# The last 21 gathers of an index-driven copy into other homes, without pacing waits, and the token rows read back after the last turned pair

## The chip, the cores and the metric
One core of one Trainium2 chip runs the whole kernel as one program. The metric is the device time of that program in microseconds (us). The engines are named PE (TensorE, matmuls and transposes), DVE (VectorE), ACT (ScalarE), POOL (GpSimd) and SP (SyncE, which here only issues transfers).

## The reference, cut to what matters
A decoder block on x of 8 sequences, 256 positions, 256 features: a linear attention, then a cross attention with a table of relative positions, then a mixture of 8 experts. The change lies in the second part. It needs, for all pairs (v, m) of positions, the table row `rpe[hops[v, m]]`, and from it one product for each head and sequence:

```
pos_emb = rpe[hops]                                   # 256 x 256 rows of 256 floats
pe = pos_emb.reshape(Sq, Sq, NH, DH)
k_hop = jnp.einsum('bhvc,vmhc->bhvm', qh, pe)
qk = jnp.einsum('bhsd,bhtd->bhst', qh, k_scaled)
C = (qk + k_hop) * D
...
x = x + _L0_xattn_ref(_layernorm(x, axis=-1), ctx_1024, ctx_1024, ...)
```

The queries come from the first part's output x, which is also added at the end (the residual) and so must be kept until then.

## The kernel before, in words
**Stages.** From 0 to about 178 us PE computes the first attention, one sequence after another (the loops over b). From about 165 to 351 us it works on the table ("pairs", below). From 351 to about 425 us it does the cross attention in 16 units of 4.5 us each (u, half the heads of one sequence), and after that the router and the experts up to 752 us.

**Gathers.** The mask needed is triangular, so the 256 x 256 table rows are packed in 257 tiles n of 128 partitions and 256 floats. POOL fetches each with one indirect DMA (`gather`, L332: "in_rpe" is the table, "hopi" the indices), in the order that `tokens_gpsimd` and the loop after it in the block set. POOL runs its instructions in order, so a gather whose wait is not met holds all that follow.

**Homes.** `rows_of(n)` says where tile n lands. There are 142 first homes: spare room in PET, U and E1 (tiles 0 to 39), 86 slots of G (40 to 125), and the 16 rows of X (126 to 141, `NKEPT`). X holds the token rows x; each pair of its rows is stored to HBM (`kept_dram`, "tokens_kept", semaphore `x_st`) before a gather may overwrite it. The tiles from 142 on reuse homes: 142 to 149 rows of U, 150 to 235 the G slots, and 236 to 256 the G slots 65 to 85 a third time. `last_in(n)` is the tile that lay in n's home before.

**Pairs.** PE turns tiles in pairs q (tiles 2q and 2q+1) with four transposes (`turn_pair`, L1031), which raise the semaphore `turned`; DVE and ACT copy them from PSUM to PET by turns, and PE multiplies them with the queries four pairs later (`products`, L2102). "turned >= k" means that pairs 0 to k-1 are turned. PE goes through pairs in order and waits for the landing of both tiles of a pair.

**Pacing.** Besides the wait for its home, each gather has a second one. In the loops over b it stands behind some step of PE (`gather_behind`); in the loop at the end of the block it waits for `turned >= min(evenly, n // 2 - LEAD)`, `evenly` being a straight line from pair 7 up.

**Tokens back.** SP waits for turned >= 71 (all tiles in X are turned), and reads X back from HBM in one DMA of 2 MB (semaphore `x_ld`). After that come in SP's order: four loads of the running maximum (`run_max`, 512 KB each, into "Dm" tiles in G), each behind a count of turned pairs; the context of two sequences; then, when the last product is done, five small loads (semaphore `m_ld`), and the loads of the cross attention.

**Who needs X and the small loads.** `mlstm_gpsimd`: POOL masks the Dm tiles (`mask(u)`, L1181), ACT takes their exponentials (`decay(u)`, L1403), DVE multiplies. Between `mask(2)` and `mask(3)` POOL waits for `x_ld` and for `m_ld` (before L1226, which changes one of the small loads); the first sum into X comes 14 us later.

Of the kernel before, what the change touches and what calls it, by code (L numbers as in the profile page):

```python
# [16 lines left out]
B, S, D = 8, 256, 256  # L17
# [24 lines left out]
NBLK = 257  # L42
# [5 lines left out]
LEAD = 6  # L48
# [66 lines left out]
def build(nc, x_d, ctx_d, ctxr_d, idx_d, cst_d, wqT_d, wkT_d, wvT_d, woT_d, wk_d, gw_d, sw_d, wg_d, gb_d,  # L115
          rpe_d, lnw_d, lnb_d, rng_d, rnb_d, rw_d, rb_d, lg_d, lb_d, w1_d, b1_d, w2_d, b2_d, out_d):
    ctx = ExitStack()
    with ctx:
# [155 lines left out]
        def rows_of(n):  # L274
# [21 lines left out]
            if n < NFULL:  # L296
                k = n - NSPARE
            elif n < NFIRST + NAGAIN + NBUF:
                k = n - NFIRST - NAGAIN
            else:  # L300
                k = THIRD_AT + n - NFIRST - NAGAIN - NBUF
# [11 lines left out]
        def last_in(n):  # L313

            if n < NFIRST + NAGAIN:
                return LATE + n - NFIRST
            if n < NFIRST + NAGAIN + NBUF:
                return n - NFIRST - NAGAIN + NSPARE
            return NFIRST + NAGAIN + THIRD_AT + n - NFIRST - NAGAIN - NBUF
# [39 lines left out]
        def tokens_gpsimd(pool):  # L359
# [19 lines left out]
            for b in range(-1, B + 1):  # L379
                new, now, old = b + 1 < B, 0 <= b < B, b >= 1  # L380
# [31 lines left out]
                if b == B:  # L412
                    for q in range(2, NTURNED - 1):
                        gather_behind(turned, q)
                if now:
                    gather_behind(av_d, NU * b + 4)
                if b == B:
                    gather_behind(qt_full, B)
# [692 lines left out]
        def mlstm_sync(sp):  # L1111
# [22 lines left out]
            context(1)  # L1134
            sp.wait_ge(prod, products_done(NPAIR - 1))
# [910 lines left out]
        with nc.Block(no_gpsimd_drain=True) as block:  # L2046
            @block.sync
            def _(sp):
                tokens_sync(sp)

                sp.wait_ge(r_M_r, 1)
                sp.dma_start(m_dram, r_M).then_inc(r_dma, 16)
                sp.wait_ge(turned, (NFIRST - 1) // 2 + 1)
                sp.dma_start(X[:, 0:NKEPT, :], kept_dram).then_inc(x_ld, 16)
                sp.wait_ge(r_dma, 16)
                mlstm_sync(sp)
                experts_sync(sp)

            @block.gpsimd
            def _(pool):  # L2060
                rest = tokens_gpsimd(pool)
                for i, n in enumerate(rest):

                    evenly = NTURNED + 1 + i * (NPAIR - LEAD - NTURNED) // len(rest)
                    if n < NFIRST:
                        pool.wait_ge(x_st, 16 * ((n - NFULL) // 2 + 1))
                        pool.wait_ge(turned, min(evenly, n // 2 - LEAD))
                    else:
                        pool.wait_ge(turned, max(last_in(n) // 2 + 1, min(evenly, n // 2 - LEAD)))
                    gather(pool, n)  # L2070
# [209 lines left out]
```

## Time and profile before

| what | us |
|---|---|
| median of 3 runs (lowest, highest) | 752.5 (751.54, 754.65) |
| time of the profiled execution | 754.1 |
| its span in the trace | 751.9 |
| PE busy in the span | 723.6 |
| POOL busy in the span | 452.3 |
| first and last gather start | 3.62 and 344.21 |

The profile's span begins at the first instruction and ends with the last. All times in the rows below are us from the span's start unless they say otherwise. PE's clock is granted by a throttle; "PEclk" of 1.00 is full speed. A row's "idle before" names what ended the idle time of that engine before the instruction; "issue" there means that the engine waited for nothing that the profile shows.

### The profile page before, as it was taken

The numbers are of one execution on the slowest core, as the hardware profiler recorded it, in microseconds if no ns is written. First come the engines' busy times: TensorE is split into PE (matmuls) and PEld (weight loads), VectorE is DVE, ScalarE is ACT, GpSimd is POOL, SyncE is SP. The second block draws the span as 40 slices with busy tenths as digits, with TensorE's granted clock in tenths as the row PEclk, the third lists the DMA queues.
The fourth block names the chain that finished last, engine by engine and source line by source line (L and its number), as shares of the span: only waits on it lengthen the run. The fifth ranks groups of instructions, "written<-read, shape, count | busy, mean of one in ns | idle before, by whom it ended". The sixth has DMA issues, their size and how long they took to land.

```text
span 751.9 us, 17208 instructions
## 1 busy us (share of the span) xinstructions
PE 723.6 (96%) x5868; PEld 652.5 (87%) x5869; DVE 394.8 (53%) x1003; ACT 365.5 (49%) x944; POOL 452.3 (60%) x522
## 2 busy tenths in 40 slices
PE   8999999988999999988999989999999999999996
PEld 4667777768999999987999966999999999999995
DVE  2567666675856534433999993333333333333331
ACT  2334444334766534435999664434434344343441
POOL 6767777776877777775776541444454444544442
PEclk8999999999999999999999999999999999999999
DMA  8434444443333375643898996121212222122221
GB/s 294 132 94 129 131 135 136 138 135 95 92 99 102 104 217 158 158 128 82 266 255 216 304 362 210 29 42 35 35 35 35 39 38 35 35 35 40 37 35 22
DMA packets 75812, 88.29 MB, mean 117 GB/s; under 512 B 11952, under 2 KB 66032, under 8 KB 75632
## 3 DMA queue, kind: packets, MB, share of 16 engines
q0 software_dynamic: 19824, 43.93, 23.9%
q1 hardware_dynamic: 52256, 40.11, 18.0%
q10 hardware_dynamic: 3680, 3.54, 1.4%
q8 instruction: 34, 0.56, 0.3%
q14 instruction: 18, 0.15, 0.1%
HBM read 75.82 MB, written 11.73 MB: 116 GB/s over the span
## 4 chain that ended last, share of the span: by engine, by line
PE 81%; issue 5%; POOL 5%; DVE 5%; DMA 3%; ACT 1%; SPq 0%; DVEq 0%; POOLq 0%; ACTq 0%
PE ps L1795 19%; PE ps L1803 18%; PE ps L2102 10%; PE ps L1031 5%; POOL G L332 4%; PE ps L485 4%; PE ps L1301 3%; PE ps L552 2%; PE ps L526 2%; PE ps L478 2%; PE ps L1303 2%; PE ps L576 1%; PE ps L450 1%; PE ps L1784 1%; PE ps L1283 1%
## 5 line engine op out<-in xcount | busy, mean ns | idle before, releaser
L332 POOL DMA_INDIRECT G<-in_rpe,hopi x193 | 188.0, 974 | 65.1 <-issue 54.0
L1860 ACT ACTIVATE G<-ps,U 128x128 f32<-128x128 f32 x312 | 84.9, 384 | 161.6 <-PE ps L1795 161.6
L1795 PEld LDWEIGHTS ps<-G,QT 128*128 128x128 f32 x1248 | 145.3, 192 | 1.9
L1795 PE MATMUL ps<-G,QT 128*128 128x128 f32 x1248 | 145.5, 275 | 0.0
L1803 PE MATMUL ps<-G 128*128 x624 | 141.0, 379 | 0.0
L1803 PEld LDWEIGHTS ps<-G 128*128 128x128 f32 x624 | 115.6, 190 | 14.2
L2102 PE MATMUL ps<-U,PET 128*128 128x128 f32 (+3 forms) x768 | 100.6, 275 | 0.0
L2102 PEld LDWEIGHTS ps<-U,PET 128*128 128x128 f32 x768 | 94.4, 194 | 0.1
L979 DVE COPY PET<-ps 128x512 f32<-128x512 f32 x64 | 44.2, 691 | 84.9 <-PE ps L1031 83.4
L1739 POOL DMA_INDIRECT out<-G,slots x39 | 71.3, 1829 | 24.0 <-issue 24.0
L2145 ACT ACTIVATE PET<-ps 128x512 f32<-128x512 f32 (+1 forms) x63 | 37.4, 594 | 84.6 <-PE ps L1031 81.1
L2007 DVE TENSOR_SCALAR G<-ps,U 128x128 f32<-128x128 f32 x78 | 28.4, 406 | 83.1 <-PE ps L1784 83.1
L1031 PE MATMUL ps<-cst,G 128*128 128x128 f32 x386 | 59.5, 277 | 4.2 <-DMA G<-in_rpe,hopi 4.2
L1716 POOL DMA_INDIRECT G<-hidden_rows,slots x39 | 40.0, 1027 | 35.1 <-issue 15.1
L1745 POOL TENSOR_TENSOR U<-cst 128x1 f32<-128x1 f32 x37 | 8.0, 215 | 85.3 <-DMA out<-G,slots 85.3
L677 ACT ACTIVATE U<-ps 128x512 f32<-128x512 f32 (+2 forms) x56 | 28.7, 512 | 55.2 <-PE ps L478 29.8
L1031 PEld LDWEIGHTS ps<-cst,G 128*128 128x128 f32 x386 | 46.3, 148 | 4.9 <-DMA G<-in_rpe,hopi 4.9
L2037 DVE SCALAR_TENSOR_TENSOR G<-ps,U,G 128x256 f32<-128x256 f32 x39 | 18.9, 484 | 59.1 <-PE ps L1803 59.1
L810 DVE TENSOR_TENSOR U<-ps,cst 128x1024 f32<-128x1024 f32 x32 | 38.3, 1219 | 13.8 <-PE ps L552 8.2
L332 POOL DMA_INDIRECT U<-in_rpe,hopi x38 | 38.3, 1007 | 11.6 <-issue 11.0
L1844 ACT ACTIVATE QT<-U 128x1024 f32 x39 | 43.2, 1109 | 2.4 <-issue 2.4
L1995 DVE TENSOR_SCALAR QT<-U 128x1024 f32 x39 | 27.1, 694 | 28.5 <-issue 28.5
(250 smaller groups left out, 1254.3 us busy)
## 6 DMA issues: line engine op xcount, KB each, us to landing
G<-run_max SPq DMA_DIRECT2D x16, 512.0 KB, 7.5
U<-in_w SPq DMA_DIRECT2D x16, 512.0 KB, 7.5
G<-in_w SPq DMA_DIRECT2D x8, 1024.0 KB, 12.4
G<-in_rpe,hopi POOLq DMA_INDIRECT x193, 2.9
U<-in_ctx SPq DMA_DIRECT2D x8, 256.0 KB, 2.8
tokens_kept<-X SPq DMA_DIRECT2D x8, 256.0 KB, 2.4
X<-tokens_kept SPq DMA_DIRECT2D x1, 2048.0 KB, 11.6
hidden_rows<-QT ACTq DMA_DIRECT2D x8, 256.0 KB, 6.8
```

Of the source, the lines that this page charges most:

```text
L332: pool.indirect_dma_start(out=dst, out_offset=None, in_=rpe_d, in_offset=bass.IndirectOffsetOnAxis(ap=hopi[:, n:n + 1], axis=0)) \
L810: nc.vector.tensor_tensor(am[n % 2], s, tri.unsqueeze(1).unsqueeze(1).to_broadcast([P, 4, 2, P]), ALU.mult).then_inc(am_r, 1)
L979: copy(PET[:, q % NPT, 0:w], bank(turn_bank(q), 512)[:, 0:w]).then_inc(pet_r[q % 2], 1)
L1031: mm = pe.transpose(o[:, n % 2, j, :], src[:, j * P:(j + 1) * P], ident)
L1716: pool.indirect_dma_start(out=z_in[u], out_offset=None, in_=z_dram, in_offset=bass.IndirectOffsetOnAxis(ap=tokg[:, u:u + 1], axis=0)) \
L1739: pool.indirect_dma_start(out=out_d, out_offset=bass.IndirectOffsetOnAxis(ap=tok[:, u:u + 1], axis=0), in_=ysb[u], in_offset=None, bounds_ ...
L1795: mm = pe.matmul(bank(1 + 2 * u + c // 4, 4, P)[:, c % 4], w1c[u][:, k, c], hT[u][:, k, :], start=(k == 0), stop=(k == KC - 1))
L1803: mm = pe.matmul(bank(6 + u, D), gel[u][:, c, :], w2s[:, one(e), c, :].rearrange("p o n -> p (o n)"), start=(c == 0), stop=(c == NI - 1))
L1844: nc.scalar.activation(w1c[u][:, 1], w1_of(e, 1), ACT.Copy) \
L1860: ins = nc.scalar.activation(gel[u][:, c, :], bank(1 + 2 * u + c // 4, 4, P)[:, c % 4], ACT.Gelu, bias=b1c[u][:, c:c + 1])
L2102: mm = pe.matmul(o, pet[:, n % 2, j, :], rhs, start=True, stop=True, skip_group_check=True)
L2145: return nc.scalar.activation(out, src, ACT.Copy)
```

## The change
It has three parts. (1) Tiles 236 to 251 land in the 16 rows of X, and only 252 to 256 in G slots (65 to 69). (2) The loop over b on POOL ends one turn earlier, so that the gathers it issued in the turn b = B come in the plain loop, and that loop has no `evenly`: a gather waits for its home alone. (3) SP reads X back after all 129 pairs are turned, behind the contexts and ahead of the five small loads.

```
             elif n < NFIRST + NAGAIN + NBUF:
                 k = n - NFIRST - NAGAIN
+            elif n < NFIRST + NAGAIN + NBUF + NKEPT:
+                return X[:, n - NFIRST - NAGAIN - NBUF, :]
             else:
-                k = THIRD_AT + n - NFIRST - NAGAIN - NBUF
+                k = THIRD_AT + n - NFIRST - NAGAIN - NBUF - NKEPT
             return G[:, k * D:(k + 1) * D]
...
             if n < NFIRST + NAGAIN + NBUF:
                 return n - NFIRST - NAGAIN + NSPARE
-            return NFIRST + NAGAIN + THIRD_AT + n - NFIRST - NAGAIN - NBUF
+            if n < NFIRST + NAGAIN + NBUF + NKEPT:
+                return NFULL + n - NFIRST - NAGAIN - NBUF
+            return NFIRST + NAGAIN + THIRD_AT + n - NFIRST - NAGAIN - NBUF - NKEPT
...
-            for b in range(-1, B + 1):
-                new, now, old = b + 1 < B, 0 <= b < B, b >= 1
+            for b in range(-1, B):
+                new, now, old = b + 1 < B, 0 <= b, b >= 1
...
-                if b == B:
-                    for q in range(2, NTURNED - 1):
-                        gather_behind(turned, q)
                 if now:
                     gather_behind(av_d, NU * b + 4)
-                if b == B:
-                    gather_behind(qt_full, B)
...
             context(0)
             context(1)
+            read_until(NBLK - 1)
+            sp.dma_start(X[:, 0:NKEPT, :], kept_dram).then_inc(x_ld, 16)
             sp.wait_ge(prod, products_done(NPAIR - 1))
...
-                sp.wait_ge(turned, (NFIRST - 1) // 2 + 1)
-                sp.dma_start(X[:, 0:NKEPT, :], kept_dram).then_inc(x_ld, 16)
...
-                for i, n in enumerate(rest):
-
-                    evenly = NTURNED + 1 + i * (NPAIR - LEAD - NTURNED) // len(rest)
+                for n in rest:
                     if n < NFIRST:
                         pool.wait_ge(x_st, 16 * ((n - NFULL) // 2 + 1))
-                        pool.wait_ge(turned, min(evenly, n // 2 - LEAD))
                     else:
-                        pool.wait_ge(turned, max(last_in(n) // 2 + 1, min(evenly, n // 2 - LEAD)))
+                        pool.wait_ge(turned, last_in(n) // 2 + 1)
                     gather(pool, n)
```

On POOL, at tiles 125 to 133, the order before is this (L332 is the gather; the names in brackets are the semaphores that it waits for, "gathered" the landing of a gather 40 tiles earlier, "gate_full" PE's last product of the first attention):

```order
L332 DMA G<-in_rpe,hopi 128x256 [waits ct_full]
L332 DMA X<-in_rpe,hopi 128x256 [waits gathered3,x_st,out_full]
L332 DMA X<-in_rpe,hopi 128x256 [waits x_st,turned]
L332 DMA X<-in_rpe,hopi 128x256 [waits gathered4,x_st,turned]
L332 DMA X<-in_rpe,hopi 128x256 [waits x_st,turned]
L332 DMA X<-in_rpe,hopi 128x256 [waits gathered5,x_st,qt_full]
L332 DMA X<-in_rpe,hopi 128x256 [waits x_st,gate_full]
L332 DMA X<-in_rpe,hopi 128x256 [waits gathered6,turned,x_st]
L332 DMA X<-in_rpe,hopi 128x256 [waits turned,x_st]
```

and of the change, the same nine tiles:

```order
L336 DMA G<-in_rpe,hopi 128x256 [waits x_st]
L336 DMA X<-in_rpe,hopi 128x256 [waits gathered3,x_st]
L336 DMA X<-in_rpe,hopi 128x256 [waits x_st]
L336 DMA X<-in_rpe,hopi 128x256 [waits gathered4,x_st]
L336 DMA X<-in_rpe,hopi 128x256 [waits x_st]
L336 DMA X<-in_rpe,hopi 128x256 [waits gathered5,x_st]
L336 DMA X<-in_rpe,hopi 128x256 [waits x_st]
L336 DMA X<-in_rpe,hopi 128x256 [waits gathered6,x_st]
L336 DMA X<-in_rpe,hopi 128x256 [waits x_st]
```

No gather has moved; the waits for PE are gone, and only those for the stored token rows stay.

On SP, from the store of the running maximum to the last small load, before (m_dram is "run_max"):

```order
L2052 DMA run_max<-U 64x256 [waits r_M_r]
L2054 DMA X<-tokens_kept 128x16x256 [waits turned]
L1127 DMA G<-run_max 128x4x256 [waits turned,r_dma]
L1127 DMA G<-run_max 128x4x256 [waits turned] x3
L1115 DMA G<-in_ctx 128x256 [waits turned]
L1116 DMA G<-in_ctxr 128x256
L1115 DMA G<-in_ctx 128x256
L1116 DMA G<-in_ctxr 128x256
L1138 DMA PET<-in_lnw 128x256 [waits prod]
L1138 DMA PET<-in_rw 128x2x8
L1138 DMA PET<-in_rng 128x2
L1138 DMA PET<-in_rnb 128x2
```

and of the change:

```order
L2053 DMA run_max<-U 64x256 [waits r_M_r]
L1126 DMA G<-run_max 128x4x256 [waits turned,r_dma]
L1126 DMA G<-run_max 128x4x256 [waits turned] x3
L1114 DMA G<-in_ctx 128x256 [waits turned]
L1115 DMA G<-in_ctxr 128x256
L1114 DMA G<-in_ctx 128x256
L1115 DMA G<-in_ctxr 128x256
L1135 DMA X<-tokens_kept 128x16x256 [waits turned]
L1139 DMA PET<-in_lnw 128x256 [waits prod]
L1139 DMA PET<-in_rw 128x2x8
L1139 DMA PET<-in_rng 128x2
L1139 DMA PET<-in_rnb 128x2
```

The 2 MB read of X went past eight loads, and now stands right ahead of the small loads.

## Rows read from the trace of the kernel before

**Rows 1.** The page: busy us and share of the span of each engine.
```profile
PE 723.6 (96%) x5868; PEld 652.5 (87%) x5869; DVE 394.8 (53%) x1003; ACT 365.5 (49%) x944; POOL 452.3 (60%) x522
```

**Rows 2.** The chain that ended last, near the last gathers (start, length, what).
```profile
336.71 0.95 POOL G L332
337.65 0.30 issue
337.96 3.85 DMA G<-in_rpe,hopi
```

**Rows 3.** POOL's instructions in order of time, at tiles 131 and 132.
```profile
177.02 1.44 POOL L332 DMA_INDIRECT X<-in_rpe,hopi  x1 [1.64 <-PE ps L596]
181.06 0.94 POOL L332 DMA_INDIRECT X<-in_rpe,hopi  x1 [2.61 <-PE ps L1031]
```

**Rows 4.** PE's instructions in order of time, at pairs 12 and 13.
```profile
187.59 0.60 PE L1031 MATMUL ps<-cst,U 128*128 128x128 f32 x4
...
188.91 0.60 PE L1031 MATMUL ps<-cst,U 128*128 128x128 f32 x4
```

**Rows 5.** PE's instructions in order of time, pairs 121 to 128.
```profile
331.53 0.66 PE L1031 MATMUL ps<-cst,G 128*128 128x128 f32 x4
...
335.69 0.66 PE L1031 MATMUL ps<-cst,G 128*128 128x128 f32 x4 [0.96 <-DMA G<-in_rpe,hopi]
...
346.09 0.63 PE L1031 MATMUL ps<-cst,G 128*128 128x128 f32 x4
...
347.45 0.38 PE L1031 MATMUL ps<-cst,G 128*128 128x128 f32 x2
```

**Rows 6.** Busy time in three stretches: PE, PEld, DVE, ACT, POOL, PEclk, DMA share, GB/s.
```profile
331.50:341.80 10.30, 6.12 (x50) 5.44 (x48) 2.09 (x4) 1.89 (x5) 7.66 (x9) 1.00 0.37 106
341.80:346.00 4.20, 4.15 (x24) 4.16 (x25) 0.69 (x1) 0.73 (x2) 3.48 (x5) 0.59 0.36 101
266.00:276.00 10.00, 10.00 (x94) 10.00 (x92) 4.37 (x7) 4.00 (x9) 7.56 (x9) 1.00 0.99 314
```

**Rows 7.** DMA issues: line or tensors, count, KB each where fixed, us from issue to landing.
```profile
G<-in_rpe,hopi POOLq DMA_INDIRECT x193, 2.9
...
X<-tokens_kept SPq DMA_DIRECT2D x1, 2048.0 KB, 11.6
out<-X SPq DMA_DIRECT2D x1, 2048.0 KB, 7.8
X<-in_x SPq DMA_DIRECT2D x1, 1536.0 KB, 16.5
out<-X SPq DMA_DIRECT2D x1, 128.0 KB, 8.6
PET<-in_rb SPq DMA_DIRECT2D x1, 4.0 KB, 2.9
```

**Rows 8.** SP's issues in order of time: start, length of the issue.
```profile
5.54 8.54 SPq L349 DMA_DIRECT2D U<-in_ctx  x1
...
177.66 0.37 SPq L357 DMA_DIRECT2D tokens_kept<-X  x1
...
353.26 0.43 SPq L1138 DMA_DIRECT2D PET<-in_rb  x1
...
451.25 0.38 SPq L1703 DMA_DIRECT2D out<-X  x1
451.68 3.09 SPq L1704 DMA_DIRECT2D out<-X  x1
```

**Rows 9.** POOL's instructions in order of time, last gather to mask(3).
```profile
344.21 0.95 POOL L332 DMA_INDIRECT G<-in_rpe,hopi  x1 [0.30 <-issue]
...
356.31 0.87 POOL L1226 TENSOR_SCALAR PET<-PET 128x256 f32<-128x256 f32 x1 [3.53 <-DMA PET<-in_rb]
357.26 2.81 POOL L1181 TENSOR_SCALAR_AFFINE_SELECT G<-G 128x512 f32<-128x512 f32 x2
```

**Rows 10.** ACT's instructions in order of time: first of decay(3).
```profile
361.50 0.50 ACT L1403 ACTIVATE G<-G,AT 128x256 f32<-128x256 f32 x1
```

## The prediction
> **What bounds the kernel now.** I read the page first: PE is busy 96% of the span, POOL 60% [rows 1]. By shares alone gathers would be free. The chain of waits says otherwise for one stage: near the end of the table stage it leaves PE and runs back through POOL, gather after gather, 0.95 us each with 0.30 us between them [rows 2]. So a tile costs POOL 1.25 us and a pair 2.5 us. PE needs less for a pair: turning pair 12 and pair 13 begins 1.32 us apart [rows 4]. PE begins far behind POOL (it turns pair 12, tiles 24 and 25, at 187.59, and POOL had begun tile 132 at 181.06 [rows 3, 4]) and catches it up at the end. In PE's own order of time this is seen from pair 122 on: it turns pair 121 at 331.53 and pair 128 at 347.45, 15.92 us for seven pairs that would take 7 x 1.32 = 9.2 us [rows 5]. The missing 6.7 us are idle time before the turns, ended by the landing of a gather, and a stretch of 4.2 us at a granted clock of 0.59, the lower of the two levels, which followed 10.3 us in which PE was busy for 6.1 [rows 6]. The last gather starts at 344.21 [rows 9], and the last turn (one tile) follows 3.2 us later. So the end of this stage moves with POOL's last gather, and what comes behind it, the cross attention, starts from there.
>
> **Part 2, the waits taken away.** I looked for every gather whose idle time is over 0.30 us and is ended by PE. In the part that the change touches there are two: tile 131, which stood 1.64 us behind gate_full, and tile 132, which stood 2.61 us behind turned >= 7 [rows 3]. All later ones, 124 of them, show 0.30 or 0.31 us: their paced waits are met when POOL comes. Taken away: (1.64 - 0.30) + (2.61 - 0.30) = 1.34 + 2.31 = 3.65 us. Do other waits step in? x_st: the last two of the 16 rows of X are stored about 180 us (SP issues that store at 177.66 [rows 8]), and their tiles 140 and 141 come eight and nine places behind tile 132, now at 181.06 - 3.65 = 177.41, so not before 177.41 + 8 x 1.25 = 187.4. Tile 142 needs turned >= 13; pair 12 is turned at 187.59 + 0.60 = 188.2, and POOL comes to that tile at 177.41 + 10 x 1.25 = 189.9 or later. From tile 150 on the need grows by one pair in two gathers (2.5 us) while PE makes a pair in 1.32 us. None of them holds POOL. So the last gather starts at 344.21 - 3.65 = 340.56. The bounds: 3.3 to 4.0, since some gathers take 1.3 to 1.6 us instead of 0.95 (tile 131 took 1.44, [rows 3]), and which ones do will be others.
>
> **Part 1, the new homes.** Before, tiles 236 to 256 waited for turned >= 108 to 118 or the pacing, and were never held. Into X they need turned >= 64 to 71, long past; tiles 252 to 256 need turned >= 108 to 110, some 20 pairs before PE's place. One gather costs the same whatever its home. This part is worth nothing by itself; 0 us. It only matters that X is now in use to the end, which forces part 3.
>
> **What PE makes of it.** PE's own pace would bring pair 128 at 331.53 + 9.24 = 340.8, the gathers bring it at 347.45 - 3.65 = 343.8: still bound by POOL, so all of the 3.65 arrives. PE now meets POOL some three pairs later and idles about 3 us rather than 6. The stretch at the low clock cost a little that showed: the last gather, with the median landing of 2.9 us [rows 7], was there at 344.21 + 2.9 = 347.1, and its turn began at 347.45 [rows 5], since PE was still at work that had piled up. If the clock holds, 0.35 more: about 4.0 us for the end of the stage.
>
> **Part 3, the tokens back late.** It now starts when pair 128 is turned: the turn ended at 347.45 + 0.38 = 347.83 before [rows 5], so 343.8 now. It lands in 7.8 us if it is like the other 2 MB transfer that ran alone, the store at the end, or in 11.6 us as this very transfer did before [rows 7], when the gathers ran beside it and the transfer engines were busy for 0.99 [rows 6]. No gather is left in flight by 343.8 + 0.5, so I take 8.0: 351.8. The five small loads come behind it on SP's queue. In the pair of stores at the end the second, of 128 KB, was held 3.09 us at its issue and landed at 451.68 + 8.6 = 460.3, 1.2 us after the first (451.25 + 7.8 = 459.05) [rows 7, 8]. So the small loads land at 351.8 + 1.2 = 353.0. Before, the last of them landed at 353.26 + 2.9 = 356.2 [rows 7, 8], 4.0 earlier would be 352.2: they are 0.8 us late. Who waits for that? POOL does L1226 and mask(3), which ended at 357.26 + 2.81 = 360.07 [rows 9]; queued behind it are the masks 4 and 5. ACT took mask(3)'s tile at 361.50 [rows 10], so 1.4 us are free. 0.8 fits in: cost 0, and I take 0.3 for the run_max loads that are also queued behind the 2 MB. If that cover were gone each us more would cost one us, since POOL, ACT, DVE and PE pass the units on in 4.5 us steps without slack. The bounds: with 11.6 us X lands at 355.4, the small loads at 356.6, 4.4 late, cost 3.0.
>
> The Trainium skill has a rule that speaks against this part: by "DMA: Bandwidth & Descriptors", section "Two DMAs through the same engine are not ordered", descriptors of one queue on one transfer engine start in order. By it the small loads cannot pass the 2 MB; the two stores at the end agree with it. Its fit in the section "Anatomy of one DMA" (2.0 us and the bytes over 436 GB/s, given for transfers issued by POOL) makes an estimate of 6.8 us for X, which would leave the small loads in time; the row's 7.8 is used.
>
> **Sum.** -3.65 (waits) - 0.35 (clock) + 0.3 (late loads) = -3.7 us. Against the profiled execution: 754.1 - 3.7 = 750.4 (span 748.2). That execution was 1.6 us above the median of the three; against the median it is 752.5 - 3.7 = 748.8.
>
> **Rivals.**
> 1. The tokens land late (as before, in 11.6 us, or SP is held at their issue): net -4.0 + 1 to 3, so 749.5 to 751.5. For it: the 8.54 us in which SP was held behind the loads at the start [rows 8]. Against it: nothing else moves then.
> 2. The clock falls where it hurts. Before, the low stretch lay where PE would have waited for gathers anyway. If PE's idle time of 3 us before pairs 126 to 128 brings such a stretch on, it lies over the last products and the first unit. Its 4.2 us at 0.59 take 0.41 x 4.2 = 1.7 us, which then all show: -3.65 + 1.7 + 0.3 = -1.65, so 750.9. Against it: the idle share is smaller than the 4.2 of 10.3 us before.
> 3. Nothing comes of it: POOL's gathers, set off against DVE's work, lose the 3.65 us again in longer ones, 752.5. Against it: the work beside them is periodic and the same.
> 4. Slower: X takes as long as the 1.5 MB of tokens at the start, 16.5 us [rows 7]. Then it lands at 360.3, the small loads at 361.5, 9.3 late, cost 7.9, net +3.9: 756.4. It decides from the point at which the small loads land over 5.4 us late (1.4 of slack and the 4.0 won), that is when X takes 12.4 us or more. Against it: at the start it shared the transfer engines with the other first loads, and now it has them nearly alone.
>
> **How the numbers follow.** Chances: the forecast 0.60, rival 1 0.16, rival 2 0.11, rival 3 0.05, rival 4 0.08. The forecast's own range is -3.0 to -4.2, with 0.7 us for the spread of medians (three runs spread over 3.1): 747.6 to 750.2. To hold 8 in 10 it must reach over most of rivals 1 and 2, so 747.4 to 752.0. A change of this kernel under 0.5% (3.8 us) can hardly be told from none. The forecast stands nearly on that line: 0.41 for faster, of the forecast a little under 0.7; within 0.5% is the rest of it with rivals 1 to 3, 0.52; slower is most of rival 4, 0.07.
>
> **What would show it.** In the profile after: no idle time over 0.3 us before the gathers of tiles 131 and 132; last gather at 340.6; pair 128 turned at some 343.5; at most three turns that wait for a gather; X issued at 343.8 and landed within 9 us; mask(3) done before ACT's decay(3) asks for it, so that the cross attention starts 4.0 us earlier. Wrong it would be if POOL showed new waits for turned or x_st, if L1226 began later than 353.8, or if PE's clock were low after 344.

## The result, and the profile after

| | before | after |
|---|---|---|
| median (lowest to highest), 6 runs each | 751.5 us (748.28 to 754.65) | 746.9 us (743.68 to 747.93) |
| profiled execution | 754.1 us | 746.76 us |
| its span | 751.9 us | 744.6 us |

The ratio on record is 0.9921, 95% interval 0.9902 to 0.9940: 5.9 us saved, between 4.5 and 7.4. The two medians of six differ by less, 4.6 us. The forecast was 748.8 us in a range of 747.4 to 752.0 and a saving of 3.7 us. The direction was right; the measured 746.9 lies 0.5 us below the range, 1.9 below the forecast. Of these 1.9 us, 1.0 is the base (the median of the kernel before was 752.5 with three runs and is 751.5 with six), and the rest a saving that was forecast too small. On two further chips, on which the kernel before itself takes 810 to 811 us, the same change costs 58 and 61 us; that is told with the experiments.

**The page.** PE is busy for 4.3 us less, POOL for as long as before; compare [rows 1].

```profile
PE 719.3 (97%) x5868; PEld 650.1 (87%) x5869; DVE 394.9 (53%) x1003; ACT 365.2 (49%) x944; POOL 452.1 (61%) x522
```

**POOL in order of time, after**: tiles 131, 132, 142, and the last gather (idle time before each in brackets).

```profile
174.07 0.95 POOL L336 DMA_INDIRECT X<-in_rpe,hopi  x1 [0.30 <-issue]
175.32 0.95 POOL L336 DMA_INDIRECT X<-in_rpe,hopi  x1 [0.30 <-issue]
...
187.82 0.95 POOL L336 DMA_INDIRECT U<-in_rpe,hopi  x1 [0.30 <-issue]
...
337.59 0.95 POOL L336 DMA_INDIRECT G<-in_rpe,hopi  x1 [0.30 <-issue]
```

The waits of 1.64 and 2.61 us of [rows 3] are gone, as announced, and no gather behind them waits. But the last gather [rows 9] comes 6.62 us earlier (344.21 - 337.59), not 3.65. Where is the other 2.97? Tile 131 stood at 177.02 with a wait of which 1.34 was removed, so 175.68 was expected for it, and it comes at 174.07: 1.61 us were won ahead of everything that the change touches. The page's windows show where: between 41 and 46 us, in the first attention, which is the same code in both kernels, PE ran at a granted clock of 0.66 in the execution before and at full clock in the one after (first row before, second after). By tile 40, at 55.96 us before and 54.37 after, the 1.6 us are complete, and they stay the same up to tile 130.

```profile
41.00:46.00 5.00, 4.36 (x25) 2.93 (x26) 2.51 (x6) 1.34 (x3) 2.98 (x4) 0.66 0.30 86
```

```profile
41.00:46.00 5.00, 4.58 (x35) 3.65 (x36) 3.77 (x9) 2.24 (x5) 3.78 (x5) 1.00 0.36 107
```

The rest, 1.36 us, is in the gathers' own length. POOL's groups over the same 132 gathers, tiles 125 or 126 to 256, before and then after (busy us, mean ns; idle us):

```profile
L332 POOL DMA_INDIRECT G<-in_rpe,hopi x108 | 107.1, 991 | 32.9 <-issue 29.9 <-PE ps L1031 3.0
L332 POOL DMA_INDIRECT X<-in_rpe,hopi x16 | 17.3, 1079 | 8.5 <-issue 3.7 <-PE ps L1031 3.2 <-PE ps L596 1.6
L332 POOL DMA_INDIRECT U<-in_rpe,hopi x8 | 9.8, 1230 | 2.4 <-issue 1.8 <-PE ps L1031 0.6
```

```profile
L336 POOL DMA_INDIRECT G<-in_rpe,hopi x92 | 92.0, 1000 | 28.0 <-issue 26.2 <-PE ps L1030 1.8
L336 POOL DMA_INDIRECT X<-in_rpe,hopi x32 | 31.7, 989 | 9.8 <-issue 9.4 <-DMA tokens_kept<-X 0.3
L336 POOL DMA_INDIRECT U<-in_rpe,hopi x8 | 9.2, 1145 | 2.4 <-issue 1.5 <-PE ps L1030 0.9
```

Before they were busy for 107.1 + 17.3 + 9.8 = 134.2 us, after for 92.0 + 31.7 + 9.2 = 132.9: 1.3 us less. The traces tell which: before, tiles 131, 138 and 139 took 1.44, 1.58 and 1.55 us, each beside an instruction of DVE (last section); after, all of tiles 127 to 141 take 0.94 to 0.96. That is 1.7 us. From tile 142 on the long gathers sit at other places, as foretold, and cost 0.4 more than before (6.9 us over 0.95 each, against 6.5). So the last gather's 6.62 is 3.65 of waits, 1.3 of shorter gathers and 1.6 from a stretch that the change doesn't touch.

**PE in order of time, after**: the turns of the last pairs and the products before them.

```profile
335.16 0.60 PE L1030 MATMUL ps<-cst,X 128*128 128x128 f32 x4
335.60 1.03 PE L2098 MATMUL ps<-U,PET 128*128 128x128 f32 x8
337.23 0.66 PE L1030 MATMUL ps<-cst,G 128*128 128x128 f32 x4 [0.60 <-DMA G<-in_rpe,hopi]
337.72 0.98 PE L2098 MATMUL ps<-U,PET 128*128 128x64 f32 x8
339.19 0.66 PE L1030 MATMUL ps<-cst,G 128*128 128x128 f32 x4 [0.48 <-DMA G<-in_rpe,hopi]
339.68 1.06 PE L2098 MATMUL ps<-U,PET 128*128 128x128 f32 x8
340.57 0.38 PE L1030 MATMUL ps<-cst,G 128*128 128x128 f32 x2
```

Two turns wait for a gather, 0.60 and 0.48 us. The last pair is turned at 340.57, 6.88 us earlier than in [rows 5]. The stretch at the low clock [rows 6] is gone from here:

```profile
336.00:340.60 4.60, 3.51 (x31) 3.24 (x31) 1.19 (x2) 1.42 (x3) 3.89 (x7) 1.00 0.31 90
340.60:345.00 4.40, 4.40 (x47) 4.26 (x49) 0.69 (x1) 3.09 (x9) 0.85 (x4) 1.00 0.60 185
```

The 6.88 is 6.62 from POOL and 0.26 from PE, for which I had 0.35.

The spans differ by 7.3 us, so that 0.4 is lost again and 0.8 won behind the table stage. The 0.4 is told next. Of the 0.8, a single wait of PE for a gather of hidden rows (L1784, L1785 after) has 0.63: 1.18 us before and 0.55 after. It lies in the experts, whose code is the same.

**The tokens back.** SP's issues, the landing of X (last figure, us), POOL's first instruction that needs the small loads, and mask(3); then ACT's decay(3):

```profile
340.98 0.38 SPq L1135 DMA_DIRECT2D X<-tokens_kept  x1
...
346.38 0.43 SPq L1139 DMA_DIRECT2D PET<-in_rb  x1
```

```profile
X<-tokens_kept SPq DMA_DIRECT2D x1, 2048.0 KB, 8.5
```

```profile
351.18 2.23 POOL L1227 TENSOR_SCALAR PET<-PET 128x256 f32<-128x256 f32 x1 [5.28 <-DMA PET<-in_rb]
353.48 1.22 POOL L1182 TENSOR_SCALAR_AFFINE_SELECT G<-G 128x512 f32<-128x512 f32 x2
```

```profile
354.74 0.51 ACT L1404 ACTIVATE G<-G,AT 128x256 f32<-128x256 f32 x1
```

X lands after 8.5 us, at 349.5; the last small load is there at 346.38 + 4.6 = 351.0, 1.5 us later, and L1227 starts 0.2 behind it. L1227 begins 5.13 us earlier than in [rows 9], the end of the table stage 6.88 earlier: the small loads are 1.75 us late against the stage. mask(3) ends at 354.70 and decay(3) begins at 354.74 [rows 10], so the cover of 1.4 us was used up and nearly nothing lost there. Over the whole cross attention 0.4 us are lost (its last matmuls, L1336, begin at 432.01 before and at 425.53 after, 6.48 earlier), where I had forecast 0.3.

### The profile page after: what moved, and what is told of

It is laid out like the page before. It is cut to its first block, busy times and chain, and to the rows that moved or that the text cites. A ratio compares the mean times of both kernels' runs of the same rounds, so it can differ in the third digit from the quotient of the medians.

```text
span 744.6 us, 17200 instructions
## 1 busy us (share of the span) xinstructions
PE 719.3 (97%) x5868; PEld 650.1 (87%) x5869; DVE 394.9 (53%) x1003; ACT 365.2 (49%) x944; POOL 452.1 (61%) x522
## 4 chain that ended last, share of the span: by engine, by line
PE 79%; POOL 7%; DVE 6%; issue 4%; DMA 2%; ACT 1%; SPq 0%; DVEq 0%; POOLq 0%; ACTq 0%
PE ps L1796 19%; PE ps L1804 18%; PE ps L2098 9%; PE ps L1030 4%; POOL G L336 4%; PE ps L484 4%; PE ps L1302 3%; PE ps L551 2%; PE ps L525 2%; PE ps L477 2%; POOL X L336 2%; PE ps L575 1%; PE ps L1304 1%; PE ps L449 1%; PE ps L1785 1%
## 5 line engine op out<-in xcount | busy, mean ns | idle before, releaser
L336 POOL DMA_INDIRECT G<-in_rpe,hopi x177 | 173.0, 977 | 58.8 <-issue 51.3
L1030 PE MATMUL ps<-cst,G 128*128 128x128 f32 x354 | 53.8, 274 | 1.1 <-DMA G<-in_rpe,hopi 1.1
L809 DVE TENSOR_TENSOR U<-ps,cst 128x1024 f32<-128x1024 f32 x32 | 38.3, 1219 | 12.4 <-PE ps L551 8.1
L1030 PEld LDWEIGHTS ps<-cst,G 128*128 128x128 f32 x354 | 42.1, 147 | 1.4 <-DMA G<-in_rpe,hopi 1.4
```

The costliest lines, as they stand in the source:

```text
L336: pool.indirect_dma_start(out=dst, out_offset=None, in_=rpe_d, in_offset=bass.IndirectOffsetOnAxis(ap=hopi[:, n:n + 1], axis=0)) \
L809: nc.vector.tensor_tensor(am[n % 2], s, tri.unsqueeze(1).unsqueeze(1).to_broadcast([P, 4, 2, P]), ALU.mult).then_inc(am_r, 1)
L1030: mm = pe.transpose(o[:, n % 2, j, :], src[:, j * P:(j + 1) * P], ident)
```

## The experiments

### The chips
The experiments ran on five numbered chips. On four of them (8, 1, 12 and 14) the kernel before takes 810 to 811 us, on one (9) it takes 752 us, as it did in the first measurement, for which no chip number is on record. I name the two kinds by these figures, "752" and "811", and every ratio is to the kernel before on the same chip. Each chip was used at one time only, so that the runs don't tell whether the chip itself makes the kind or something around it. Of the change's own figure on the 752 kind there is one measurement, the first.

The traces do tell where the two kinds part. In the kernel before, tile 125 begins at 167.46 us on the 752 kind and at 195.93 on the 811 kind, 28.5 later; the last gather at 344.21 and 398.86, 54.7 later; and from there to the end it takes 407.7 and 408.9 us. So nearly all of the 56 us by which these spans differ (751.9 and 807.8) arise in the stretch with gathers, the first attention included.

### The terms of the sum, one at a time (811)
**Waits for homes alone, without new homes and late tokens.** `rows_of` and the place of X as before, POOL's loop as changed:

```
-            elif n < NFIRST + NAGAIN + NBUF + NKEPT:
-                return X[:, n - NFIRST - NAGAIN - NBUF, :]
...
+                sp.wait_ge(turned, (NFIRST - 1) // 2 + 1)
+                sp.dma_start(X[:, 0:NKEPT, :], kept_dram).then_inc(x_ld, 16)
```

> Part 2 alone: gathers wait for their homes only, but the third homes are the G slots and the tokens are read back at turned >= 71, both as before. Theory W (the two waits of 3.65 us on POOL, with what follows for the clock at the end of the stage, are the whole gain): the stage ends some 5 to 6.5 us earlier than before in the trace, less a stall of about 0.5 us before tile 236, which now comes at 312 and needs turned >= 108; the cross attention then loses nothing to late tokens (0.4 us in the changed kernel). Time within 0.5 us of the changed kernel, 5 to 6 us under before. Rival T (moving the 2 MB read out of the middle of the table stage, and the X homes, bring a part of the gain): 2 us or more slower than the changed kernel.

Measured: 871.1 us, ratio 1.0715 (1.0665 to 1.0766).

**The two waits put back.**

```
                 for n in rest:
+                    if n == NFULL + 5:
+                        pool.wait_ge(gate_full, B)
+                    if n == NFULL + 6:
+                        pool.wait_ge(turned, NTURNED + 1)
```

> The changed kernel with just the two waits put back that stood idle before: gate_full before tile 131, turned >= 7 before tile 132. Theory W: last gather 3.65 us later by the waits and about 1.3 us more by gathers that again meet DVE's work, so 4.5 to 5.5 us slower than the changed kernel, and again a stretch at the low clock near 340; nearly the time of before. Rival T: at most 3 us slower than the changed kernel, 2 us or more faster than before.

Measured: 862.6 us, 1.0627 (1.0569 to 1.0684).

**The tokens behind the small loads**, with POOL's wait for them moved to just before the first sum into X:

```
-            sp.dma_start(X[:, 0:NKEPT, :], kept_dram).then_inc(x_ld, 16)
             sp.wait_ge(prod, products_done(NPAIR - 1))
...
+            sp.dma_start(X[:, 0:NKEPT, :], kept_dram).then_inc(x_ld, 16)
```

> The changed kernel with the 2 MB read issued behind the five small loads instead of ahead of them, and POOL waiting for it only before the first sum into X. Theory W: the small loads land 2.3 to 2.9 us after their issue as before, mask(3) is no longer late, 0.1 to 0.5 us faster than the changed kernel, hardly to be told from it. If the later run_max loads now queue behind the 2 MB and hold mask(4) or mask(5), up to 2 us slower.

Measured: 873.3 us, 1.0738 (1.0688 to 1.0788).

**The tokens after the last product, ahead of the small loads.**

> The changed kernel with the 2 MB read issued after the last product, 3.5 us later, still ahead of the small loads. The cover (the time until ACT asks for mask(3)'s tile) was used up by then in the changed kernel: mask(3) ended 0.04 us before ACT began on it. So each us later should cost one: 3.3 to 3.7 us slower than the changed kernel. If POOL's lateness were made good within the 16 units, under 1 us slower.

Measured: 872.1 us, 1.0749 (1.0696 to 1.0801). All four expectations were missed, since the ground under them was another: a loss of 51 to 62 us, in which terms of 0.3 to 4 us can't be read.

Two of the texts that follow say that PE stood still "for want of instructions". The trace shows no more than that it waited for nothing that the profile knows; see "Left open" below.

**The changed kernel itself and three of the four again, on chip 1.**

> The changed kernel itself, to stand beside the others on one chip. In the four runs so far, on another chip than the first measurement, the kernel before took 811 us, not 752, and the edited kernels 863 to 873: PE stood still there for want of instructions in the stretches in which gathers ran. If this chip is like the first, 5 to 6 us under before. If it is like the second, some 872 us beside 811, as in the run with the waits alone.

Measured: 868.8 us, 1.0719 (1.0676 to 1.0762).

> Part 2 alone, as in the first of the runs so far. On a chip like that of the first measurement, theory W: within 0.5 us of the changed kernel. Rival T (the 2 MB read out of the middle and the X homes bring a part): 2 us or more slower than the changed kernel. On a chip like the second, both theories silent: some 870 us.

Measured: 871.7 us, 1.0730 (1.0686 to 1.0775).

> The changed kernel with the waits before tiles 131 and 132 put back. On a chip like that of the first measurement, theory W: 4.5 to 5.5 us slower than the changed kernel and nearly the time of before. Rival T: at most 3 us slower than the changed kernel.

Measured: 865.7 us, 1.0678 (1.0641 to 1.0714).

> The changed kernel with the 2 MB read behind the five small loads, and POOL waiting for it before the first sum into X alone. 0.1 to 0.5 us faster than the changed kernel; up to 2 us slower if the later run_max loads are held by it.

Measured: 869.2 us, 1.0712 (1.0676 to 1.0748). So part 2 alone has the whole loss, and the place of the tokens makes no difference there that the runs can tell.

### Where the 58 us go (811)
The kernel before, with its profile:

> The kernel before, for its profile on a chip where it takes 811 us. There the changed kernel stood still on PE for want of instructions in stretches of 10 to 20 us while gathers ran without a break, and ran at full speed while POOL waited. Theory P (the pacing that was taken away let PE recover: a gather that waits for PE stops the gathers as soon as PE is late): in before's profile POOL shows many short waits for turned in the table stage, and PE's stretches without instructions are shorter and fewer, by some 58 us in all. Rival Q (the place of the 2 MB read or the X homes cost the 58 us): POOL shows no more waits than in the changed kernel.

Measured: 810.0 us, span 807.8, one run. Here is PE in order of time in the changed kernel (chip 1), and under it POOL at the same time ("remote" marks a wait whose releaser the trace doesn't have on this core):

```profile
298.44 0.37 PE L1030 MATMUL ps<-cst,G 128*128 128x128 f32 x1 [0.81 <-issue]
299.84 0.47 PE L1030 MATMUL ps<-cst,G 128*128 128x128 f32 x1 [1.03 <-issue]
300.54 0.37 PE L1030 MATMUL ps<-cst,G 128*128 128x128 f32 x1 [0.23 <-issue]
302.64 0.37 PE L1030 MATMUL ps<-cst,G 128*128 128x128 f32 x1 [1.73 <-issue]
...
306.68 1.06 PE L1030 MATMUL ps<-cst,G 128*128 128x128 f32 x4
```

```profile
300.43 0.95 POOL L336 DMA_INDIRECT G<-in_rpe,hopi  x1 [0.30 <-issue]
301.69 0.94 POOL L336 DMA_INDIRECT G<-in_rpe,hopi  x1 [0.31 <-issue]
305.73 0.95 POOL L336 DMA_INDIRECT G<-in_rpe,hopi  x1 [3.10 <-remote]
```

PE does a single matmul and stands for about 1 us "<-issue": no landing, no semaphore, nothing that the profile shows. It recovers at 305 to 307, when POOL has paused for 3.10 us. Nor does the standstill come at once: POOL's gathers run without a break from 273.86 on, and PE still turns a pair each 1.3 us up to 286.3. The waits between 180 and 460 us, the changed kernel and then the one before (us in total, times, longest):

```profile
PE ps L2098 <- issue: 28.3, 42, 1.5
```

```profile
POOL G L332 <- PE ps L1031: 19.9, 16, 5.2
PE ps L2102 <- issue: 14.4, 25, 1.6
```

The same idle time is there before, half as much (with the turns, L1030 and L1031, PE has 42.5 us of it in the changed kernel and 17.7 in the one before), and POOL is held 16 times for pairs that PE has not turned: on this chip the paced waits do hold POOL, which on the other they never did behind tile 132 [rows 3]. Windows of 20 us show what that is worth. The columns are PE, PEld, DVE, ACT and POOL (each busy us and instructions), PE's clock, the DMA share, GB/s; the changed kernel, then the one before:

```profile
240.00:260.00 20.00, 15.22 (x100) 12.97 (x100) 8.95 (x17) 6.77 (x16) 13.44 (x14) 0.83 0.34 96
280.00:300.00 20.00, 12.87 (x85) 10.85 (x84) 3.98 (x7) 3.91 (x9) 15.43 (x16) 0.77 0.38 104
400.00:420.00 20.00, 20.00 (x185) 20.00 (x185) 8.27 (x14) 9.30 (x18) 0.00 (x0) 1.00 0.18 54
```

```profile
240.00:260.00 20.00, 17.76 (x153) 16.93 (x153) 9.50 (x16) 9.84 (x22) 13.27 (x14) 1.00 0.30 88
280.00:300.00 20.00, 17.59 (x153) 16.87 (x152) 9.51 (x17) 10.56 (x23) 12.94 (x14) 1.00 0.31 92
```

With 16 gathers in 20 us PE gets through 85 matmuls, with 14 and a pause every four or five 153, with none 185. The mean number is not all: 14 gathers stand beside 100 matmuls in one kernel and beside 153 in the other. None is at 400 to 420 because POOL is then held for its home for 44.63 us (tile 252). On the 752 chip PE gets through 184 or 185 beside 16 gathers. In the changed kernel the clock falls as well, after PE's idle time, and its part is large: from 200 to 400 us it is 0.77 in the mean, where it is 0.97 in the kernel before on that kind. By my estimate, 200 x (0.97 - 0.77), the lower clock stands for up to 40 us, and the added idle time for 25; they overlap, since the clock is also low while PE stands. Three kernels test it. **Parts 1 and 3 alone**, all of POOL's waits as before:

> Parts 1 and 3 alone: tiles 236 to 251 into X and the tokens back after the last turned pair, all of POOL's waits as before. Theory P: the time of before within 3 us. Rival Q: near that of the changed kernel, some 869 us beside 811.

Measured: 809.6 us, 0.9978 (0.9951 to 1.0005): no difference that the runs can tell, and none of the loss.

**Half the pacing**, from tile 142 on:

```
+                    i = n - NFULL + 1
+                    evenly = NTURNED + 1 + i * (NPAIR - LEAD - NTURNED) // (NBLK - NFULL + 1)
...
+                        home = last_in(n) // 2 + 1
-                        pool.wait_ge(turned, last_in(n) // 2 + 1)
+                        pool.wait_ge(turned, max(home, (home + min(evenly, n // 2 - LEAD)) // 2))
```

> The changed kernel with, for tiles from 142 on, a wait for a count of turned pairs halfway between the home's and that of before. Theory P: between the two, 825 to 855 us beside 811. Rival Q: as the changed kernel, 869.

Measured: 845.7 us, 1.0414 (1.0364 to 1.0463), between the two, as expected.

**A gap before each gather** from tile 142 on, with no wait for PE: POOL fills a small tile.

```
+                    if n >= NFIRST:
+                        nc.gpsimd.memset(gap[:, :], 0.0).then_inc(zeros, 1)
+                        pool.wait_ge(zeros, n - NFIRST + 2)
```

> The changed kernel with a small memset on POOL ahead of each gather from tile 142 on (256 elements a partition, some 0.2 us, and the hop to itself), so that gathers come at most every 1.6 to 1.8 us instead of 1.25. If PE starves by the rate of the gathers, 20 to 50 us faster than the changed kernel's 869. If what helps is that POOL stops when PE is late, and not the rate, no gain of more than 10 us. On a chip like that of the first measurement it would be 45 to 60 us slower, bound by POOL.

Measured: 828.3 us, 1.0192 (1.0144 to 1.0240). Its windows:

```profile
240.00:260.00 20.00, 20.00 (x183) 19.76 (x182) 14.63 (x26) 13.49 (x30) 16.74 (x25) 1.00 0.29 80
280.00:300.00 20.00, 20.00 (x185) 20.00 (x184) 11.59 (x21) 12.58 (x26) 16.75 (x25) 1.00 0.28 79
```

This is the sharpest of the runs. POOL has more work and no wait for PE is put back, and PE is back at its full pace, 183 to 185 matmuls, with no "<-issue" between 230 and 420 us and a clock of 1.00 in these windows. Gathers that begin 1.56 us apart leave PE alone; unbroken ones 1.25 us apart do not. Whether the longer distance does it, or the 0.6 us of other work between two gathers, is not told apart. The kernel is still slower than before, since POOL is now the bound: its last gather starts at 417.88, 19 us later than in the kernel before on that chip (398.86), and the span is 19.1 longer.

### The pacing and POOL's rate (752)
The first of three kernels keeps the pacing, but only from tile 142 on:

```
-                        pool.wait_ge(turned, last_in(n) // 2 + 1)
+                        evenly = NTURNED + 1 + (n - NFULL - 6) * (NPAIR - LEAD - NTURNED) // (NBLK - NFULL - 6)
+                        pool.wait_ge(turned, max(last_in(n) // 2 + 1, min(evenly, n // 2 - LEAD)))
```

> The changed kernel, but each gather from tile 142 on also waits for the same number of turned pairs as in the kernel before (the straight line from pair 7 up, never closer than 6 pairs); the gathers of tiles 126 to 141 stay free of waits for PE. If what costs the 55 to 60 us on these chips is that POOL no longer pauses from tile 142 on, this kernel takes 808 to 814 us beside 811 for the one before (ratio 0.995 to 1.005), and the two waits at tiles 131 and 132 are then worth 0 to 5 us here as well. Rival (the early gathers beside the end of the first attention do the harm): 860 or more. PE's idle time ended by nothing that the profile shows falls from 28 to about 14 us in the matmuls of the table stage by the first, and stays at 28 by the second.

This was measured on a chip of the 752 kind, for which the figures above were not made. Measured: 749.6 us beside 752.2, 0.9961 (0.9945 to 0.9978). By the ratios that is a saving of 2.9 us where the change saves 5.9, by the medians 2.6 where it saves 4.6. POOL in order of time:

```profile
186.92 0.95 POOL L336 DMA_INDIRECT X<-in_rpe,hopi  x1 [0.30 <-issue]
191.14 0.94 POOL L336 DMA_INDIRECT U<-in_rpe,hopi  x1 [3.27 <-PE ps L1030]
192.47 0.94 POOL L336 DMA_INDIRECT U<-in_rpe,hopi  x1 [0.39 <-PE ps L1030]
193.80 1.23 POOL L336 DMA_INDIRECT U<-in_rpe,hopi  x1 [0.39 <-PE ps L1030]
...
340.44 0.95 POOL L336 DMA_INDIRECT G<-in_rpe,hopi  x1 [0.30 <-issue]
```

The time won at tiles 131 and 132 is lost again at tile 142, in a new wait of 3.27 us (with the two behind it 3.15 over the usual 0.30): freed POOL arrives before PE has turned enough pairs. So the 3.65 us of waits belong to both halves of part 2 together; with the pacing in place 0.5 of them would have come. From tile 125 to the last gather this kernel takes 174.25 us, the one before 176.75 and the changed one 171.75. The 2.5 us against before are those 0.5 and 1.9 of shorter gathers: tiles 131, 138 and 139 take 0.95 us here too.

**A pause before each fourth gather** (four fillings), and **twice the gap before each** (two fillings), no pacing:

> The changed kernel with no wait for turned pairs put back; instead POOL fills a small tile four times (4 x 0.33 us and their hops, some 2.4 us) ahead of every fourth gather from tile 142 on. The work added is the same as in the run with one filling ahead of each gather (828 us, ratio 1.019). If POOL's mean rate of gathers sets the harm, this kernel takes 825 to 832 as that one did. If pauses long enough for PE to be served matter, it takes 812 to 820. If short gaps everywhere are what helps, it is worse: 835 to 850.

Measured: 788.7 us, 1.0471 (1.0437 to 1.0505).

> The changed kernel with two fillings of the small tile (some 1.2 us) ahead of each gather from tile 142 on, where the earlier run had one (0.6 us, 828 us). A tile then costs POOL about 2.15 us, a pair 4.3 us, against 1.32 for PE's turn alone and about 2.6 for a pair as these chips run the kernel before. If the rate is what matters, PE's idle time without a reason goes away, but POOL becomes late: from 230 us on 115 tiles take 247 us, so the table stage would end at about 480 instead of 400 and the kernel takes 860 to 890. Should the stage end earlier than POOL's rate says, this reasoning on rates is wrong.

Measured: 833.7 us, 1.1070 (1.1041 to 1.1099). Both expectations were made for the 811 kind, so the question of the first, whether pauses help PE there or the rate does, was not answered. Here the two show something cleaner, the price of POOL's rate:

| kernel, 752 | last gather starts | span | difference |
|---|---|---|---|
| changed | 337.59 | 744.6 | 407.0 |
| paced from 142 | 340.44 | 748.0 | 407.6 |
| before | 344.21 | 751.9 | 407.7 |
| pause each fourth | 379.96 | 787.2 | 407.2 |
| gaps twice | 422.82 | 831.8 | 409.0 |

Over 85 us of shift the span follows the last gather to within 2 us. That the table stage ends with POOL's last gather on the 752 kind is thus shown, and a microsecond there is one of the kernel. In the last kernel PE waits for landings and its granted clock sinks to near the lower level:

```profile
360.00:380.00 20.00, 12.70 (x61) 11.48 (x60) 2.47 (x4) 3.10 (x6) 15.60 (x30) 0.59 0.23 66
```

### The two waits and part 2 alone, once more (811)
The three expectations have a figure for either kind; the chip was one of the 811 kind, so that the two waits and the tokens remain unsized on the 752 kind.

> The changed kernel itself, beside the kernel before on the same chip. Where the kernel before takes 752 us, 745 to 748 us, ratio 0.990 to 0.995, with POOL's last gather near 337.6; where it takes 811 us, 866 to 872 and ratio 1.07. It is the base for the other two runs of this call.

Measured: 871.7 us, 1.0742 (1.0705 to 1.0778).

> The changed kernel with the two waits that stood at tiles 131 and 132 put back, homes alone from there on. Where the kernel before takes 752 us: my sum gives these waits 3.65 us, so POOL's last gather comes at 341 to 342 and the kernel takes 3 to 4 us more than the changed one in the same call, ratio 0.995 to 1.000 to before. Rival (the time comes from elsewhere, the waits only move to later ones): within 1 us of the changed kernel. Where the kernel before takes 811 us: less than the changed one by 3 to 6 us, as in the two earlier calls.

Measured: 863.7 us, 1.0632 (1.0597 to 1.0668).

> Part 2 alone: the waits for homes alone, with the old third homes and the tokens read back at turned >= 71, as before. Where the kernel before takes 752 us: by the theory that part 3 costs 0.3 to 0.4 us through late small loads and part 1 saves at most 0.5, it takes the same as the changed kernel, within 0.8 us. Rival (the new place of X pays, since the 2 MB no longer run beside the gathers): 1 us or more above the changed kernel. Where the kernel before takes 811 us: the same as the changed kernel, within 3 us.

Measured: 871.5 us, 1.0724 (1.0688 to 1.0761). With the two waits put back the kernel is faster there by 8.0 us (and by 3.1 on chip 1), where 3 to 6 were expected. Part 2 alone again takes the same as the whole change.

## Why the prediction came out as it did

- **What bounds the kernel**: right on the 752 kind, and shown by the table above. On the 811 kind the changed kernel's span is 425.4 us longer than the start of its last gather (864.3 and 438.87), not 407 to 409: there PE is behind.
- **Part 2, the step that failed**: the removed waits are gone and nothing holds POOL behind them; the 3.65 us stand. What failed is the size of this term, by its bound: "3.3 to 4.0, since some gathers take 1.3 to 1.6 us instead of 0.95". I had the long gathers move to other places at the same cost. But tile 131's 1.44 us, which I quoted, and the 1.58 and 1.55 of tiles 138 and 139 went with the waits: from tile 125 to the last gather POOL takes 171.75 us instead of 176.75, so the term measured 5.0, of which 3.65 are waits and 1.3 gathers. (In excess of 0.95 us each, the 132 gathers cost 8.9 us before, 7.6 after and 7.0 in the kernel paced from tile 142 on.) Tiles 127 to 141 were all short in each of the four traces on the 752 kind in which they run without PE's waits, and the excess from tile 142 on was 6.5 before, 6.9 after and 6.3 in the paced kernel. So the 1.7 us at the early tiles look like a part of the change that comes back, and the 0.4 lost behind them can't be told from chance.
- **Against the median**: 1.6 of the 7.3 us by which the spans differ lie ahead of the change, under the stretch of low clock near 43 us. Without them and without the 0.8 behind the cross attention the change is worth 5.0 + 0.3 - 0.4 = 4.9 us by this pair of traces, 1.2 above my 3.7, beside 4.6 by the medians of six and 5.9 (4.5 to 7.4) by the ratio. The stretch is in the one trace of the kernel before on the 752 kind and in none of the four of changed kernels. That it comes and goes by chance is likely, since the code there is the same, but it is not shown: no second trace of the kernel before was taken on that kind. That the measured median fell out of the range is also owed to the base, by 1.0 us.
- **Part 1, worth 0**: nearly right. In the old homes tile 236 would have waited for pair 107, which at the new pace is turned at about the time at which POOL comes: 0.5 us at most, worked out from the trace and not tried on the 752 kind.
- **PE, 0.35 from the clock**: 0.26, with a clock of 1.00 in the two windows from 336 to 345 us.
- **Part 3, 0.3**: X took 8.5 us instead of 8.0, the small loads came 1.5 instead of 1.2 behind it, 1.7 late instead of 0.8. The 1.4 us of cover took up most of it, and 0.4 was lost. The rule of the Trainium skill that I weighed ("DMA: Bandwidth & Descriptors", section "Two DMAs through the same engine are not ordered") agrees with the trace here: the small loads, issued at 344.55 and later, landed behind the 2 MB. The page orders the starts on each transfer engine alone and nothing across the 16, so it does not promise the order of the landings. The estimate of 6.8 us for X by the page's fit was too short by 1.7.
- **Rivals**: 1, 2 and 4 did not come about on the 752 kind. Of 3, the change in the length of the gathers came with the other sign. In rival 4 the time of X from which it decides comes to 12.6 us by its own figures (343.8 + 12.6 + 1.2 = 357.6, which is 5.4 behind 352.2), not 12.4.
- **What no rival had**: a chip on which PE stands still beside unbroken gathers. I wrote of the later gathers that "their paced waits are met when POOL comes", and put the pacing at nothing by that. It is right for the trace that I had. The cover was PE's pace of 1.32 us a pair, and its price where that cover is gone is 58 to 61 us. The trace of before could not show it, as no paced wait behind tile 132 was unmet there.
- **Left open**: why the chips differ, and what PE lacks. That PE is short of instructions is a guess from "<-issue" and from its recovery when POOL rests. The Trainium skill ("Runtime: NRT & Kernel Launch", section "Instruction fetch mechanics") says that an engine's sequencer fetches its instructions itself by DMA in blocks and that the cost is mostly hidden. The trace speaks against late blocks as the cause. In the changed kernel on the 811 kind PE stands 32 times for 22.4 us in all between 300 and 380 us, and in these 80 us the instruction queue brings two blocks of 16 KB (PE's waits in that window, then the queue's count, MB and share):

```profile
PE ps L2098 <- issue: 14.0, 21, 1.5
PE ps L1030 <- issue: 8.4, 11, 1.7
...
q8 instruction: 2, 0.03, 0.2%
```

Over the whole kernel it brings 34 such blocks on either kind. What else could hold PE, no run tested. Nor is the effect of the early gathers on the 811 kind (3 to 8 us) explained.

## What to carry to other kernels
A wait that is met in every row of a profile has a price of zero only at that pace. Before taking it out, look at how far the engine behind it would run ahead and what both share. Where one of two waits is taken out, ask whether the next stops the same engine (3.15 of 3.65 us came back at tile 142 while the pacing stood). Read the price of a producer's rate by slowing it on purpose: where it is the bound, the span moves one for one, as it did over 85 us here. Measure on more than one chip when a change lets an engine run without pauses. The change takes 0.9921 on the one kind and 1.07 on the other. The kernel paced from tile 142 on takes 0.9961 on the one, and may be safe on the other; it was not tried there.

## What the runs showed of the hardware
- The same kernel takes 752 us on one numbered chip and 810 to 811 on four others, and the change has ratios of 0.992 and 1.072 to 1.074. In the kernel before, only 1.2 of the 56 us between the spans arise behind the last gather.
- On the 811 kind, unbroken gathers 1.25 us apart hold up matmuls that wait for none of them: 85 to 100 in the two windows of 20 us shown, 153 with a pause every four or five, 183 to 185 at 1.56 us apart. The lower clock that follows PE's idle time is part of the first figure.
- A DVE instruction with two inputs in SBUF (TENSOR_TENSOR) holds up a gather that it overlaps near its start. Of the changed kernel on the 752 kind, two gathers on POOL, and then the DVE instruction beside each; the first began 0.29 us ahead of its gather, the second 0.14 us behind:

```profile
193.17 1.52 POOL L336 DMA_INDIRECT U<-in_rpe,hopi  x1 [0.30 <-PE ps L1030]
...
203.17 1.96 POOL L336 DMA_INDIRECT G<-in_rpe,hopi  x1 [0.30 <-issue]
```

```profile
192.88 1.04 DVE L2202 TENSOR_TENSOR U<-QT,cst 128x512 f32<-128x512 f32 x1
...
203.31 1.04 DVE L2202 TENSOR_TENSOR U<-QT,cst 128x512 f32<-128x512 f32 x1
```

The first gather ends at 194.69, 0.77 us after its DVE instruction (193.92), the second at 205.13, 0.78 us after its own (204.35). The same holds for every gather from tile 133 on that takes over 1.0 us in the two traces before and after: 47 of them, 1.02 to 1.98 us long, end 0.76 to 0.80 us after such an instruction (L2202, L2206 before), whenever they began. Where it begins 0.40 us or more after the gather, the gather takes its usual 0.94 or 0.95 (23 cases). Two rows after don't fit: tiles 132 and 141 took 0.95 us, though such an instruction began 0.02 and 0.11 us behind them. So it looks as if a gather that is held gets no further than its first 0.2 us until DVE is done; that is an inference, and no run took the DVE work away. The Trainium skill ("SBUF — State Buffer", section "Who interferes with whom") says that a DVE instruction with two SBUF inputs contends with a GpSimd instruction that reads SBUF; these rows agree, if a gather counts as one (its indices lie in SBUF). The same section infers that such an instruction leaves the making of descriptors alone, and there the rows differ.
